# The experts' second layer in half-precision parts, and where its weights and the first biases are loaded

## The chip, the cores and the metric

The kernel runs on one core of one Trainium2 chip. The metric is device time in microseconds (us) of one execution, as the median of several. The engines are TensorE (PE; PEld is its weight load), VectorE (DVE), ScalarE (ACT), GpSimd (POOL) and SyncE (SP), which here only issues DMAs.

## The reference

Rows of 256 numbers (3327 of them, padded to 26 tiles of 128) pass through an attention over an adjacency matrix, a feed-forward with a capacity per expert, an aggregation over the same adjacency, and a layer of eight experts, of which every row uses two. Each part reads a normalised x and adds to x. What matters here is the last layer:

```python
def _L1_ffn_ref(x, Wg, bg, W1, b1, W2, b2):
    B, S, D, DFF, E, K = (4, 1024, 256, 512, 8, 2)
    logits = jnp.einsum('bsd,de->bse', x, Wg) + bg
    topk_vals, topk_idx = jax.lax.top_k(logits, K)
    topk_w = jax.nn.softmax(topk_vals, axis=-1)
    ...
    h = jnp.einsum('bsd,edf->bsef', x, W1) + b1
    a, g = jnp.split(h, 2, axis=-1)
    act = jax.nn.silu(a) * g
    expert_out = jnp.einsum('bsef,efd->bsed', act, W2) + b2
    return jnp.einsum('bse,bsed->bsd', weights_per_expert, expert_out)
```

## The kernel before

Four stretches follow each other on the core. **Attention** fills 0 to 405 us and is not touched. **`capacity_ffn`** fills 405 to 624 us. It is written out as slots: in slots 0 to 51 (chunk c is slot // 4, 13 chunks of two 128-row tiles' work) every engine does its part of the feed-forward, and from slot 32 on a `row_work(slot)` is placed between, which normalises x, turns it and projects it (`project_row`, `turn_rows`, `normalise_row`, `row_moments`); slots 52 to 68 hold row work alone, one row tile a slot. On the side this stretch finds a scale for the experts' first weights: ACT loads each expert's W1 (`expert_load`, 1024 KB) into the buffers `W` that are free by then and squares it with a sum (`expert_square`, L926), one expert in each of chunks 2 to 9; the largest sum gives `w_scale` near the end (`expert_sums` at slot 60, `expert_scales` at slot 63).

**`aggregation_and_experts`** opens with the aggregation, 624 to about 795 us: 44 products a row tile in half precision, fed by large loads of the adjacency and of the expert weights. ACT issues the loads of the experts' W2 (`weight_load`), SP those of the first biases b1, two each at i = 20, 22 and 24 of 26, and the rest with b2 behind them. Then each row is scattered to two slots of a table in DRAM (`slot_rows`, on POOL), and 59 tiles of 128 slots are read back.

The **expert tile loop** (820 us to the end) works on three tiles at once. Its order is each engine's own code, `iteration(s, u)`, with semaphores between; tiles 0 to 5 and the last are unrolled, those between run in a loop of two tiles a round, whose turn (a branch) falls into every other tile. In iteration s

- PE does the first layer of tile s (12 products of 512 columns, L1597, "hid"), turns the rows of tile s+1 (L1586), turns the activations of tile s-1 (L1607) and does the second layer of tile s-2 (L1617), which is in fp32: four products, each recorded as two instructions;
- DVE computes `weight` and `place_i` for tile s-3 (L1762, L1765), takes hid into `hb` with the bias (L1769), makes the rest xT_lo of tile s+1 (L1753), and multiplies `act = silu * gate` (L1776);
- ACT makes xT_hi of tile s+1 (L1460), copies the turned activations of tile s-1 out of PSUM (L1469), computes silu (L1473) and tanh (L1474) of tile s, and scales the bias and the output of tile s-3 (L1479, L1482);
- POOL adds those two (L1837) and stores 128 rows by index, adding to the output in DRAM (L1842); each such store waits for the one before it to land.

In the profile many buffers of this block carry the name of the memory they lie in: `X`, `own_H`, `adj_room`, `PS`.

Of the kernel before, what the change touches and what calls it, by code (L numbers as in the profile page):

```python
# [7 lines left out]
ALU = mybir.AluOpType  # L8
# [630 lines left out]
def capacity_ffn(nc, t, dram):  # L639


    with ExitStack() as ctx:
# [59 lines left out]
        held = [w1, w2]  # L702
        eps = sb("eps", [P, 1])
        e_sq, e_sum = sb("e_sq", [P, E1]), sb("e_sum", [P, 1])
        e_root, e_floor, e_rec = (sb(n, [P, 1]) for n in ("e_root", "e_floor", "e_rec"))
        e_in = [sem(f"c_ein{u}") for u in range(2)]
        e_squared, e_summed = sem("c_esq"), sem("c_esum")
        e_rooted, e_scaled = sem("c_eroot"), sem("c_escale")
        wsn_in, wsn_hi, wsn_lo, wsn_scaled = sem("c_wsn"), sem("c_wsnhi"), sem("c_wsnlo"), sem("c_wsnscale")
# [10 lines left out]
        SLOTS, SUMS_AT = PROJECT_AT + T, 60  # L720
# [5 lines left out]
        def pair_at(slot, offset):  # L726
            return [(slot - offset) // 2] if 0 <= slot - offset < T and (slot - offset) % 2 == 0 else []

# [5 lines left out]
        def _(sp):  # L734
# [15 lines left out]
            sp.wait_ge(later_in, 80)  # L750

# [22 lines left out]
        def _(pe):  # L774
# [83 lines left out]
            def project_row(i):  # L858
                r, s = i // 2, i % 2
                if i == 0:  # L860
                    pe.wait_ge(keep_done, len(GR))
                    pe.wait_ge(wsn_lo, 1)
# [9 lines left out]
            for slot in range(SLOTS):  # L872
# [14 lines left out]
                    if slot == SUMS_AT:  # L887
                        pe.wait_ge(y_taken, NCH - 1)
                        pe.wait_ge(e_squared, E1)
                        nc.tensor.matmul(psY[NCH % 2][:, 0:E1], unit[:, :], e_sq[:, :], start=True,  # L890
                                         stop=True).then_inc(e_summed, 1)
# [12 lines left out]
        def _(act):  # L904
# [10 lines left out]
            def expert_load(e):  # L915
                if e < 2:
                    act.wait_ge(w_lo, e + 1)
                else:
                    act.wait_ge(e_squared, e - 1)
                act.dma_start(held[e % 2][:, :, :].rearrange("p k n -> p (k n)"),  # L920
                              dram["eW1"][:, e, :]).then_inc(e_in[e % 2], 16)

            def expert_square(e):
                act.wait_ge(e_in[e % 2], 16 * (e // 2) + 16)
                flat = held[e % 2][:, :, :].rearrange("p k n -> p (k n)")
                nc.scalar.activation(flat, flat, ACT.Square, accum_out=e_sq[:, e:e + 1]).then_inc(e_squared, 1)  # L926

# [18 lines left out]
            def row_work(slot):  # L946
# [4 lines left out]
                for g, (_, b) in enumerate(RG):  # L951
                    if slot == ROWS_AT + b + 1:
                        row_deviation(g)

# [40 lines left out]
            for c in range(NCH):  # L995
# [17 lines left out]
                gelu_hi(c, 2)  # L1013
                row_work(4 * c + 2)
# [5 lines left out]
            for slot in range(4 * NCH, SLOTS):  # L1020
                row_work(slot)
                if slot == SUMS_AT + 2:
                    act.wait_ge(e_scaled, 1)
                    nc.scalar.activation(e_root[:, :], e_sum[:, :], ACT.Sqrt).then_inc(e_rooted, 1)

        @block.vector
        def _(dve):
# [60 lines left out]
            def row_work(slot):  # L1088
# [9 lines left out]
                for i in row_at(slot, ROWS_AT + 1):  # L1098
                    row_moments(i)

            def expert_sums():
                dve.wait_ge(e_summed, 1)
                v.tensor_reduce(e_sum[:, :], psY[NCH % 2][:, 0:E1], AX_X, ALU.max).then_inc(e_scaled, 1)

            def expert_scales():
                dve.wait_ge(e_rooted, 1)
                v.tensor_scalar(e_floor[:, :], e_root[:, :], TINY, None, ALU.max).then_inc(e_scaled, 1)
                dve.wait_ge(e_scaled, 2)
                v.reciprocal(e_rec[:, :], e_floor[:, :]).then_inc(e_scaled, 1)
                v.tensor_scalar(t["w_unscale"][:, :], e_floor[:, :], 1.0 / (FULL * H_SCALE), None, ALU.mult).then_inc(e_scaled, 1)  # L1110
                dve.wait_ge(e_scaled, 4)
                v.tensor_scalar(t["w_scale"][:, :], e_rec[:, :], FULL, None, ALU.mult).then_inc(e_scaled, 1)
# [144 lines left out]
            for slot in range(4 * NCH, SLOTS):  # L1257
# [5 lines left out]
                if slot == SUMS_AT:  # L1263
                    expert_sums()
                if slot == SUMS_AT + 3:
                    expert_scales()


def aggregation_and_experts(nc, t, dram, out):


    with ExitStack() as ctx:
# [40 lines left out]
        W2 = room[:, 0:E1 * KF * D].rearrange("p (e k d) -> p e k d", e=E1, k=KF)  # L1313
# [6 lines left out]
        actT = [carve(KF * P).rearrange("p (k n) -> p k n", k=KF) for _ in range(2)]  # L1320
# [34 lines left out]
        weight_waits = sem("f_weight_waits")  # L1355
# [582 lines left out]
```

## Time and profile before

| | |
|---|---|
| median of three executions | 1146.9 us (1146.87, 1149.44, 1146.9) |
| profiled execution, its own time | 1146.19 us |
| its span | 1144.4 us |
| busy: PE, DVE, ACT, POOL | 1020.9, 757.1, 610.4, 354.6 us |
| granted clock of PE, mean | 0.949 of full |

The span is the time between the first and the last recorded instruction; the execution's own time has 1.8 us more around it. Busy times add up the instructions of an engine, so an engine with a low share can still be the one that all wait for in one stretch.

### The profile page before, as it was taken

To read this page: it belongs to the slowest core of one execution; us is meant where nothing else is said; L and a number is where in the kernel's file an instruction comes from. 1 tells how busy PE (TensorE), PEld (TensorE's weight loads), DVE (VectorE), ACT (ScalarE), POOL (GpSimd) and SP (SyncE) were. 2 spreads that over 40 slices of the span, in tenths; PEclk is the share of its full clock that TensorE was granted. 3 is DMA by queue.
4 is the path that set the end of the run, shared out by engine and by line. 5 is a ranking of instruction groups with operands and counts; after the bars stand their busy time and mean duration, and the time that the engine had idled before them with its cause. 6 is when DMAs were issued, how large, how long until landed. Compare 5 with 4: busy or idle time off the path is not lost. (4 is left out here: it accounts for less than half of the span.)

```text
span 1144.4 us, 23391 instructions
## 1 busy us (share of the span) xinstructions
PE 1020.9 (89%) x7604; PEld 821.5 (72%) x7605; DVE 757.1 (66%) x1636; ACT 610.4 (53%) x923; POOL 354.6 (31%) x337
## 2 busy tenths in 40 slices
PE   5749999999999699798987999998399999999991
PEld 4539989998999579687754888887166666666661
DVE  5599999999993364865665566766355555555550
ACT  2767878787873477767642212112145555555541
POOL 0233232222322000009231044433224444444443
PEclk9759999999999689999999999999599999999996
DMA  9998787878720311220061799998523333333322
GB/s 373 243 287 251 229 254 223 256 223 260 221 87 1 115 74 38 80 81 26 1 119 47 186 241 239 243 244 264 215 38 52 55 55 48 53 55 55 48 45 23
DMA packets 72845, 161.64 MB, mean 141 GB/s; under 512 B 7376, under 2 KB 58960, under 8 KB 66768
## 3 DMA queue, kind: packets, MB, share of 16 engines
q1 hardware_dynamic: 48928, 97.85, 26.9%
q0 software_dynamic: 18128, 40.17, 20.0%
q10 hardware_dynamic: 5728, 22.81, 5.5%
q8 instruction: 38, 0.62, 0.2%
q14 instruction: 23, 0.19, 0.1%
HBM read 137.47 MB, written 45.49 MB: 160 GB/s over the span
## 5 line engine op out<-in xcount | busy, mean ns | idle before, releaser
L577 PE MATMUL PS<-G,PT 128*128 128x256 f16 x2028 | 234.4, 273 | 0.0
L577 PEld LDWEIGHTS PS<-G,PT 128*128 128x128 f16 x2028 | 198.9, 98 | 22.5
L1597 PE MATMUL PS<-W,X 128*128 x708 | 164.1, 382 | 4.3 <-DVE X L1753 4.3
L1769 DVE SCALAR_TENSOR_TENSOR own_H<-PS,w_unscale,own_H 128x1024 f32<-128x1024 f32 x59 | 75.7, 1284 | 97.8 <-PE PS L1597 97.8
L1597 PEld LDWEIGHTS PS<-W,X 128*128 128x128 f16 x708 | 69.5, 98 | 84.0 <-issue 7.4
L1523 PE MATMUL PS<-own_H,adj_room 128*128 128x256 f16 x572 | 129.3, 272 | 0.0
L1521 PE MATMUL PS<-own_H,adj_room 128*128 128x257 f16 x572 | 129.3, 273 | 0.0
L1617 PE MATMUL PS<-adj_room,X 128*128 x472 | 111.6, 380 | 0.2 <-issue 0.2
L561 PE MATMUL PS<-ident,probs 128*128 128x128 f32 x676 | 91.8, 283 | 21.1 <-ACT probs L321 15.8
L406 DVE SCALAR_TENSOR_TENSOR score<-S2low,S1low,S2row 128x3327 f32<-128x3327 f32 x25 | 106.5, 4260 | 0.0
L1842 POOL DMA_INDIRECT out_dram<-X,place_i x59 | 92.3, 1564 | 28.1 <-POOL X L1837 19.9
L561 PEld LDWEIGHTS PS<-ident,probs 128*128 128x128 f32 x676 | 79.1, 146 | 26.6 <-issue 17.6
L310 ACT CAST PT<-PS 128x1024 f16<-128x1024 f32 (+1 forms) x78 | 61.9, 795 | 62.8 <-PE PS L561 62.8
L424 DVE CUSTOM_DVE_ANT_0 score<-score,maskbias 128x3327 f32<-128x3327 f32 x25 | 90.6, 3625 | 5.4 <-DVE score L406 5.2
L1837 POOL TENSOR_TENSOR X<-X 128x256 f32<-128x256 f32 x59 | 44.3, 751 | 159.5 <-ACT X L1482 152.5
L1617 PEld LDWEIGHTS PS<-adj_room,X 128*128 128x128 f32 x472 | 85.1, 190 | 9.7 <-issue 0.4
L1460 ACT ACTIVATE X<-PS 128x256 f16<-128x256 f32 x59 | 22.7, 384 | 123.2 <-PE PS L1586 123.2
L321 ACT ACTIVATE probs<-score,shift_by 128x3327 f32<-128x3327 f32 x26 | 79.9, 3073 | 8.3 <-POOL shift_by L254 8.3
L1050 DVE SCALAR_TENSOR_TENSOR c_G_lo<-c_G,c_g_scale,c_G_hi 128x512 f16<-128x512 f32 x52 | 41.2, 793 | 61.8 <-ACT c_G_hi L967 61.6
L430 DVE TENSOR_TENSOR PT<-PS,PT 128x1024 f16<-128x1024 f32 (+1 forms) x78 | 73.2, 943 | 10.1 <-ACT PT L310 10.1
L316 ACT ACTIVATE maskbias<-adjf,big 128x3327 bf16<-128x3327 f32 x26 | 79.9, 3074 | 0.0
L800 PE MATMUL c_psH<-W 128*128 128x256 f16 x624 | 78.9, 278 | 0.0
(280 smaller groups left out, 1854.4 us busy)
## 6 DMA issues: line engine op xcount, KB each, us to landing
adjf<-adj_dram SPq DMA_DIRECT2D x26, 1664.0 KB, 8.0
slot_rows<-blank SPq DMA_DIRECT2D x26, 1032.0 KB, 11.1
adj_room<-adjT_dram POOLq DMA_DIRECT2D x22, 832.0 KB, 10.5
W<-eW_dram ACTq DMA_DIRECT2D x8, 1024.0 KB, 4.7
adj_room<-eW_dram ACTq DMA_DIRECT2D x8, 1024.0 KB, 9.3
X<-slot_rows SPq DMA_DIRECT2D x59, 129.0 KB, 2.5
own_H<-eb_dram SPq DMA_DIRECT2D x8, 512.0 KB, 5.9
adj_room<-eW_dram ACTq DMA_DIRECT2D x8, 512.0 KB, 8.7
```

The lines of the kernel that those rows point to most:

```text
L316: nc.scalar.activation(bias[u][:, 0:N], adjf[u][:, 0:N], ACT.Relu, bias=big[:, :], scale=-EDGE_SCALE).then_inc(mask_ready, 1)
L321: nc.scalar.activation(probs[u][:, 0:N], score[u][:, 0:N], ACT.Exp, bias=shift_by[u][:, :], accum_out=total[u][:, :]).then_inc(probs_ready, 1)
L406: v.scalar_tensor_tensor(score[u][:, 0:N], S2low[:, 0:N], S1low[:, ds(t, 1)], S2row[:, 0:N], ALU.add, ALU.max).then_inc(leaky_ready, 1)
L424: v.tensor_tensor_reduce(score[u][:, 0:N], score[u][:, 0:N], bias[u][:, 0:N], 1.0, -2 * FAR, ALU.subtract, ALU.max, rowmax[u][:, :]).then_ ...
L561: mm = nc.tensor.transpose(psT[g % 3][:, (j - a) * P:(j - a + 1) * P], probs[u][:, j * P:(j + 1) * P], ident[:, :])
L577: mm = nc.tensor.matmul(acc[u][:, 0:D], left, right, start=(j == 0 and n == 0), stop=(j == T - 1 and n == 2))
L800: mm = nc.tensor.matmul(psH[b % 2][:, (m % 2) * CH:(m % 2 + 1) * CH], w1p[left][:, k, m * P:(m + 1) * P], HT[right][:, k, c * CH:(c + 1) * ...
L1521: nc.tensor.matmul(acc[u][:, 0:D + 1], left, H[:, j, 0:D + 1], start=(j == 0), stop=False, skip_group_check=True)
L1523: mm = nc.tensor.matmul(acc[u][:, 0:D], left, H[:, j, D + 2:2 * D + 2], start=False, stop=(j == T - 1), skip_group_check=True)
L1597: mm = nc.tensor.matmul(psHE[u][:, n * F1:(n + 1) * F1], left[u][:, k, :], W1[:, e, k, part, n * F1:(n + 1) * F1], start=(m == 0), stop=(m ...
L1617: mm = nc.tensor.matmul(psY[u][:, 0:D], actT[u][:, k, :], W2[:, e, k, :], start=(k == 0), stop=(k == KF - 1))
L1842: pool.indirect_dma_start(out=out, in_=ys[u][:, :], in_offset=None, out_offset=bass.IndirectOffsetOnAxis(ap=place_i[:, s:s + 1], axis=0), ...
```

## The change

It has three parts.

1. In the expert tile loop the second layer is done in half-precision parts: W2 and the activations are each a sum of two f16 numbers, and y = hi·hi + lo·hi + hi·lo is 12 products of 256 columns in place of four in fp32. For the activations' range each row of a tile is divided by its own size: ACT squares `hb` with a sum, DVE turns that into `size` and `rsize`, act is multiplied by `rsize`, DVE makes the rest `actT_lo`, and the output is scaled by `y_scale` (weight times size) in place of `weight`.
2. In `capacity_ffn` ACT also loads and squares W2 (four loads of two experts), two loads and squares a chunk in chunks 2 to 7; the scales are found at slots 36 to 43; and W2 of the eight experts is split into its two parts (`second_weight_hi` on ACT at slot 45 + 3e, `second_weight_lo` on DVE one slot later, the last at slot 67), which SP stores to DRAM, 512 KB each. SP waits for those stores before the stretch ends.
3. In the aggregation b1 is loaded one expert at a time at i = 2, 6, 10, 14, 18 and 22; W2 is read from the parts, in as many bytes.

```diff
+        E_LOADS = E1 + E1 // 2
...
-        SLOTS, SUMS_AT = PROJECT_AT + T, 60
+        SLOTS, SUMS_AT, SPLIT_AT = PROJECT_AT + T, 36, 45
...
+            sp.wait_ge(e_squared, E_LOADS)
+            for e in range(2):
+                sp.dma_start(raw2[e], dram["eW2"][:, e, :, :].rearrange("p k d -> p (k d)")).then_inc(raw2_in[e], 16)
+            for e in range(E1):
+                u = e % 2
+                sp.wait_ge(second_lo, e + 1)
+                sp.dma_start(dram["W2_parts"][:, e, :, :], parts2[u][:, :, :]).then_inc(parts2_out[u], 16)
+                if e + 2 < E1:
+                    sp.dma_start(raw2[u], dram["eW2"][:, e + 2, :, :].rearrange("p k d -> p (k d)")).then_inc(raw2_in[u], 16)
+            for u in range(2):
+                sp.wait_ge(parts2_out[u], 16 * (E1 // 2))
...
+            def second_weight_hi(e):
+                act.wait_ge(raw2_in[e % 2], 16 * (e // 2) + 16)
+                act.wait_ge(e_scaled, 5)
+                wait(act, parts2_out[e % 2], 16 * (e // 2))
+                nc.scalar.activation(parts2[e % 2][:, 0, :], raw2[e % 2], ACT.Copy,
+                                     scale=t["w2_scale"][:, :]).then_inc(second_hi, 1)
...
-                if 2 <= c < 2 + E1:
-                    expert_square(c - 2)
-                if 3 <= c < 1 + E1:
-                    expert_load(c - 1)
+                if 2 <= c < 2 + E_LOADS // 2:
+                    expert_square(2 * c - 4)
                 gelu(c, 2)
                 gelu_hi(c, 1)
                 row_work(4 * c + 1)
                 gelu(c, 3)
                 gelu_hi(c, 2)
+                if 2 <= c < 2 + E_LOADS // 2:
+                    expert_square(2 * c - 3)
...
+            def second_weight_lo(e):
+                dve.wait_ge(second_hi, e + 1)
+                v.scalar_tensor_tensor(parts2[e % 2][:, 1, :], raw2[e % 2], t["w2_scale"][:, :], parts2[e % 2][:, 0, :],
+                                       ALU.mult, ALU.subtract).then_inc(second_lo, 1)
...
-                if i >= 20:
-                    for e in range(i - 20, i - 18):
-                        sp.dma_start(b1[:, e, :], dram["eb1"][:, e, :]).then_inc(b1_in, 16)
+                if i % 4 == 2:
+                    e = i // 4
+                    sp.dma_start(b1[:, e, :], dram["eb1"][:, e, :]).then_inc(b1_in, 16)
...
+                    nc.scalar.activation(squares, hb[u][:, :], ACT.Square, accum_out=sumsq[u][:, :]).then_inc(squared, 1)
                     nc.scalar.activation(silu[u][:, :], hb[u][:, 0:F1], ACT.Silu).then_inc(silu_ready, 1)
...
-                    settled(act, weight_waits, (y_ready, s - 2))
+                    settled(act, weight_waits, (y_ready, s - 2), (y_scaled, s - 2))
                     nc.scalar.activation(yw[1 - u][:, :], psY[1 - u][:, 0:D], ACT.Copy,
-                                         scale=weight[:, ds(s - 3, 1)]).then_inc(yw_ready, 1)
+                                         scale=y_scale[:, ds(s - 3, 1)]).then_inc(yw_ready, 1)
...
                     for k in range(KF):
-                        mm = nc.tensor.matmul(psY[u][:, 0:D], actT[u][:, k, :], W2[:, e, k, :], start=(k == 0),
-                                              stop=(k == KF - 1))
+                        for n, (left, part) in enumerate(((actT_hi, 0), (actT_lo, 0), (actT_hi, 1))):
+                            mm = nc.tensor.matmul(psY[u][:, 0:D], left[u][:, k, :], W2[:, e, part, k, :],
+                                                  start=(k == 0 and n == 0), stop=(k == KF - 1 and n == 2))
...
+                    dve.wait_ge(weighed, s - 2)
+                    dve.wait_ge(size_kept, s - 2)
+                    v.tensor_tensor(y_scale[:, ds(s - 3, 1)], weight[:, ds(s - 3, 1)], sizes[:, ds(s - 3, 1)],
+                                    ALU.mult).then_inc(y_scaled, 1)
...
+                if due(s - 1):
+                    dve.wait_ge(actT_ready, s)
+                    wait(dve, y_ready, s - 3)
+                    v.tensor_tensor(actT_lo[1 - u][:, :, :].rearrange("p k n -> p (k n)"), psA[:, :],
+                                    actT_hi[1 - u][:, :, :].rearrange("p k n -> p (k n)"), ALU.subtract).then_inc(actT_lo_ready, 1)
...
+                    dve.wait_ge(squared, s + 1)
+                    v.tensor_scalar(size[u][:, :], sumsq[u][:, :], 1.0 / (2 * FULL), TINY * TINY, ALU.mult,
+                                    ALU.max).then_inc(sized, 1)
+                    dve.wait_ge(sized, s + 1)
+                    v.reciprocal(rsize[u][:, :], size[u][:, :]).then_inc(act_scaled, 1)
                     dve.wait_ge(silu_ready, s + 1)
+                    dve.wait_ge(act_scaled, s + 1)
                     wait(dve, a_turned, s - 1)
-                    v.tensor_tensor(act_sb[u][:, :], silu[u][:, :], hb[u][:, F1:2 * F1], ALU.mult).then_inc(act_ready, 1)
+                    v.scalar_tensor_tensor(act_sb[u][:, :], silu[u][:, :], rsize[u][:, :], hb[u][:, F1:2 * F1], ALU.mult,
+                                           ALU.mult).then_inc(act_ready, 1)
+                    v.tensor_scalar(sizes[:, ds(s, 1)], size[u][:, :], t["w2_unscale"][:, :], None, ALU.mult).then_inc(size_kept, 1)
```

The order of DVE's instructions in one tile of the expert tile loop, before: `own_H` is hb or its target, the first `X` under it xT_lo, the last act.

```order
L1762 TENSOR_SCALAR weight<-balance 128x1
L1765 TENSOR_SCALAR place_i<-kept 128x1
L1769 ISA
L1769 SCALAR_TENSOR_TENSOR own_H<-PS,w_unscale,own_H 128x1024
L1751 TENSOR_SCALAR kept<-X 128x2
L1753 SCALAR_TENSOR_TENSOR X<-PS,X 128x256
L1776 TENSOR_TENSOR X<-X,own_H 128x512
```

And in the changed kernel, the same engine and the same place:

```order
L1815 TENSOR_SCALAR weight<-balance 128x1
L1818 TENSOR_SCALAR place_i<-kept 128x1
L1821 TENSOR_TENSOR y_scale<-weight,sizes 128x1
L1826 ISA
L1826 SCALAR_TENSOR_TENSOR own_H<-PS,w_unscale,own_H 128x1024
L1804 TENSOR_SCALAR kept<-X 128x2
L1806 SCALAR_TENSOR_TENSOR X<-PS,X 128x256
L1833 TENSOR_TENSOR X<-PS,X 128x512
L1837 TENSOR_SCALAR size<-sumsq 128x1
L1840 RECIPROCAL rsize<-size 128x1
L1844 SCALAR_TENSOR_TENSOR X<-X,rsize,own_H 128x512
L1846 TENSOR_SCALAR sizes<-size,w_unscale 128x1
```

One small operation stands ahead of hb, three operations between xT_lo and act, and one behind act.

ACT's instructions in one tile of the same loop, before: the first two `X` are xT_hi and the activations' copy, the third is silu.

```order
L1460 ACTIVATE X<-PS 128x256
L1469 COPY X<-PS 128x512
L1473 ACTIVATE X<-own_H 128x512
L1474 ACTIVATE balance<-kept 128x1
```

And in the changed kernel:

```order
L1511 ACTIVATE X<-PS 128x256
L1520 CAST X<-PS 128x512
L1524 ACTIVATE rows,sumsq<-own_H 128x1024
L1525 ACTIVATE X<-own_H 128x512
L1526 ACTIVATE balance<-kept 128x1
```

The square of all 1024 columns of hb stands between hb and silu.

DVE's instructions at slots 58 and 59 of `capacity_ffn`, before: `own_H` are projected rows, `c_r_h` is a normalised row on its way to PE, `c_rowT_lo` a turned one.

```order
L1083 SCALAR_TENSOR_TENSOR own_H<-c_psR,own_H 128x256
L1085 SCALAR_TENSOR_TENSOR own_H<-c_psR,c_own_back,c_own_bias 128x256
L1069 RECIPROCAL c_row_rstd<-c_row_std 128x2
L1073 TENSOR_SCALAR c_r_h<-X,c_moments,c_row_rstd 128x256
L1061 BN_STATS stats<-X 128x6
L1063 BN_AGGR c_moments<-stats 128x2
L1083 SCALAR_TENSOR_TENSOR own_H<-c_psR,own_H 128x256
L1085 SCALAR_TENSOR_TENSOR own_H<-c_psR,c_own_back,c_own_bias 128x256
```

And in the changed kernel, where the lower part of one expert's W2 stands between the two slots:

```order
L1118 SCALAR_TENSOR_TENSOR own_H<-c_psR,own_H 128x256
L1120 SCALAR_TENSOR_TENSOR own_H<-c_psR,c_own_back,c_own_bias 128x256
L1104 RECIPROCAL c_row_rstd<-c_row_std 128x2
L1108 TENSOR_SCALAR c_r_h<-X,c_moments,c_row_rstd 128x256
L1096 BN_STATS stats<-X 128x6
L1098 BN_AGGR c_moments<-stats 128x2
L1160 SCALAR_TENSOR_TENSOR W<-W,w_scale 128x1024
L1118 SCALAR_TENSOR_TENSOR own_H<-c_psR,own_H 128x256
L1120 SCALAR_TENSOR_TENSOR own_H<-c_psR,c_own_back,c_own_bias 128x256
```

DVE has one operation more, and the next slot's two projected rows come behind it.

## Rows read from the trace of the kernel before

**Rows 1.** Windows: busy us (x instructions) of PE, PEld, DVE, ACT, POOL; clock, DMA share, GB/s

```profile
900.00:950.00 50.00, 50.00 (x263) 33.15 (x262) 26.84 (x60) 25.64 (x60) 23.09 (x21) 1.00 0.34 53
```

**Rows 2.** The chain that ended last, 899 to 912: start, us, what

```profile
901.22 1.73 PE PS L1617 x8
902.95 2.59 PE PS L1597 x12
905.54 0.22 PE PS L1586 x2
905.76 0.44 PE PS L1607 x4
```

**Rows 3.** Timeline of PE and DVE at the loop's start, tiles 0 to 2

```profile
822.05 4.36 PE L1597 MATMUL PS<-W,X 128*128 x12 [1.25 <-DVE X L1753]
...
831.32 1.28 DVE L1769 SCALAR_TENSOR_TENSOR own_H<-PS,w_unscale,own_H 128x1024 f32<-128x1024 f32 x1 [2.07 <-PE PS L1597]
...
836.06 1.28 DVE L1769 SCALAR_TENSOR_TENSOR own_H<-PS,w_unscale,own_H 128x1024 f32<-128x1024 f32 x1 [2.07 <-PE PS L1597]
```

**Rows 4.** Timeline of DVE, then ACT, two tiles of the loop

```profile
900.72 1.28 DVE L1769 SCALAR_TENSOR_TENSOR own_H<-PS,w_unscale,own_H 128x1024 f32<-128x1024 f32 x1 [1.63 <-PE PS L1597]
902.70 0.69 DVE L1776 TENSOR_TENSOR X<-X,own_H 128x512 f32<-128x512 f32 x1 [0.30 <-ACT X L1473]
904.06 0.15 DVE L1762 TENSOR_SCALAR weight<-balance  x1 [0.67 <-issue]
905.79 1.28 DVE L1769 SCALAR_TENSOR_TENSOR own_H<-PS,w_unscale,own_H 128x1024 f32<-128x1024 f32 x1 [1.41 <-PE PS L1597]
907.86 0.69 DVE L1776 TENSOR_TENSOR X<-X,own_H 128x512 f32<-128x512 f32 x1 [0.38 <-ACT X L1473]
908.72 0.15 DVE L1762 TENSOR_SCALAR weight<-balance  x1 [0.17 <-issue]
910.67 1.28 DVE L1769 SCALAR_TENSOR_TENSOR own_H<-PS,w_unscale,own_H 128x1024 f32<-128x1024 f32 x1 [1.63 <-PE PS L1597]
...
902.04 0.63 ACT L1473 ACTIVATE X<-own_H 128x512 f32<-128x512 f32 x1 [0.19 <-DVE own_H L1769]
```

**Rows 5.** The chain that ended last, 600 to 640: one product of 256 columns

```profile
626.43 0.11 PE PS L1521
```

**Rows 6.** Timeline of ACT: a square with its sum, and the operation behind it

```profile
460.71 1.90 ACT L926 ACTIVATE W<-W 128x2048 f32<-128x2048 f32 x1
...
462.60 0.56 ACT L959 ACTIVATE c_G<-c_psH,c_b,c_w_back 128x256 f32<-128x256 f32 x1
```

**Rows 7.** Timeline of POOL: the last stores of the loop

```profile
1124.17 1.56 POOL L1842 DMA_INDIRECT out_dram<-X,place_i  x1 [2.74 <-DMA out_dram<-X,place_i]
...
1128.74 1.56 POOL L1842 DMA_INDIRECT out_dram<-X,place_i  x1 [2.25 <-DMA out_dram<-X,place_i]
```

**Rows 8.** Groups of instructions: busy us, mean ns, idle before

```profile
L1152 DVE SCALAR_TENSOR_TENSOR W<-W,c_w_scale 128x2048 f16<-128x2048 f32 x2 | 4.7, 2346 | 0.8 <-ACT W L988 0.8
```

**Rows 9.** Timeline of DVE in the slots of row work, and the next block's first

```profile
609.34 0.42 DVE L1083 SCALAR_TENSOR_TENSOR own_H<-c_psR,own_H 128x256 f16<-128x256 f32 x1 [1.15 <-ACT own_H L943]
...
622.75 0.48 DVE L1085 SCALAR_TENSOR_TENSOR own_H<-c_psR,c_own_back,c_own_bias 128x256 f32<-128x256 f32 x1
624.41 0.06 DVE L1629 MEMSET eps<- 128x1 f32 x1 [1.18 <-PEq L71]
```

**Rows 10.** DMA issues: KB each, median us to landing

```profile
W<-eW_dram ACTq DMA_DIRECT2D x8, 1024.0 KB, 4.7
X<-slot_rows SPq DMA_DIRECT2D x59, 129.0 KB, 2.5
```

**Rows 11.** Windows as in rows 1, in the feed-forward's chunks and the row work

```profile
450.00:460.00 10.00, 10.00 (x94) 9.09 (x94) 3.02 (x5) 6.68 (x13) 0.00 (x0) 1.00 0.12 48
...
600.00:620.00 20.00, 15.24 (x76) 7.27 (x75) 15.84 (x47) 6.70 (x18) 2.37 (x4) 1.00 0.00 1
```

**Rows 12.** The chain that ended last, 800 to 840: the hand-over's scatter

```profile
811.53 5.36 DMA slot_rows<-rows,slot_i
```

More of the change, by code:

```diff
@@ L708, in capacity_ffn @@
         e_rooted, e_scaled = sem("c_eroot"), sem("c_escale")
+        raw2_in, parts2_out = ([sem(f"c_{n}{u}") for u in range(2)] for n in ("raw2", "parts2"))
+        second_hi, second_lo = sem("c_second_hi"), sem("c_second_lo")
         wsn_in, wsn_hi, wsn_lo, wsn_scaled = sem("c_wsn"), sem("c_wsnhi"), sem("c_wsnlo"), sem("c_wsnscale")
@@ L727, in pair_at, with split_at @@
             return [(slot - offset) // 2] if 0 <= slot - offset < T and (slot - offset) % 2 == 0 else []
+        def split_at(slot):
+            e = (slot - SPLIT_AT) // 3
+            return [e] if slot >= SPLIT_AT and (slot - SPLIT_AT) % 3 == 0 and e < E1 else []
         def fronts(c):
@@ L953, in row_work @@
                         row_deviation(g)
+                if slot == SUMS_AT + 5:
+                    act.wait_ge(e_scaled, 2)
+                    nc.scalar.activation(e_root[:, :], e_sum[:, :], ACT.Sqrt).then_inc(e_rooted, 1)
+                for e in split_at(slot):
+                    second_weight_hi(e)
             def gelu(c, b):
@@ L1099, in row_work @@
                     row_moments(i)
+                if slot == SUMS_AT + 1:
+                    expert_sums()
+                if slot == SUMS_AT + 7:
+                    expert_scales()
+                for e in split_at(slot - 1):
+                    second_weight_lo(e)
             def expert_sums():
                 dve.wait_ge(e_summed, 1)
[L1103 removed]
+                v.tensor_reduce(e_sum[:, 0:1], psR[0][:, 0:E1], AX_X, ALU.max).then_inc(e_scaled, 1)
+                v.tensor_reduce(e_sum[:, 1:2], psR[0][:, E1:E_LOADS], AX_X, ALU.max).then_inc(e_scaled, 1)
             def expert_scales():
@@ L1319, in aggregation_and_experts @@
         silu, act_sb = ([carve(F1) for _ in range(2)] for _ in range(2))
-        actT = [carve(KF * P).rearrange("p (k n) -> p k n", k=KF) for _ in range(2)]
+        actT_hi, actT_lo = ([carve(KF * P, F16).rearrange("p (k n) -> p k n", k=KF) for _ in range(2)] for _ in range(2))
+        squares = rows[:, :, :, :, :].rearrange("p q u k n -> p (q u k n)")[:, 0:2 * F1]
+        sumsq, size, rsize = ([sb(f"{n}{u}", [P, 1]) for u in range(2)] for n in ("sumsq", "size", "rsize"))
+        sizes, y_scale = sb("sizes", [P, NS]), sb("y_scale", [P, NS])
         yw, bw, ys = ([carve(D) for _ in range(2)] for _ in range(3))
```

63 lines of the change are left out of this document (35 added, 28 removed).

## The prediction

> **What bounds the kernel now.** I read the page's engines and slices first, then windows over each stretch, then in each the chain of what released what, and last the timelines of the engines that meet there. The change touches three of the four stretches.
>
> In the expert tile loop PE is never idle: 50.00 us of the window's 50, at full granted clock [rows 1]. The chain that ended last is PE's own order, tile after tile: 1.73 for the second layer, 2.59 for the first, 0.22 and 0.44 for the turns, 4.98 us a tile [rows 2]. The reader should see that this is a full PE and not a stall. But two loops through other engines run beside it, nearly as long, and they are found only by adding up starts.
>
> Loop one: hb, xT_lo of the next tile, its first layer, its hb. At the start, where tile 2's iteration has only just begun to add a second layer and PE is idle before hb for nothing but this, hb follows hb after 836.06 - 831.32 = 4.74 us [rows 3]. It holds DVE's 1.8 and PE's first layer and nothing of the second layer, so no cheaper second layer shortens it.
>
> Loop two: hb, silu, act, the small operations for tile s-3, hb. Two hb lie 910.67 - 900.72 = 9.95 us apart for two tiles, 4.97 a tile, and before each DVE waited for PE, 1.41 and 1.63 us [rows 4]. So loop two has a slack of about 1.5 us a tile: its own length is 3.66 in the tile that carries the loop's turn and 3.25 in the other.
>
> In `capacity_ffn`'s chunks PE is full too, with ACT busy 6.68 of 10 us [rows 11]. In its last slots it is not: PE 15.24 of 20, DVE 15.84 of 20 [rows 11], and DVE's only idle time is some 1.15 us in every pair of row tiles, ahead of one projected row [rows 9]. The end of the stretch is set by DVE's last row at 622.75 + 0.48, and the next block starts at 624.41 [rows 9]. In the hand-over after the aggregation the chain runs through scatters that take 5.36 us each [rows 12] while the DMA engines are busy.
>
> **The tile loop, part by part.** *Removed:* 1.73 us a tile of fp32 products [rows 2]. *Added on PE:* 12 products of 256 columns at the 0.11 us at which one follows the other on the chain [rows 5], 1.32 us. PE's own work becomes 2.59 + 0.22 + 0.44 + 1.32 = 4.57 us, 0.41 less; over 56 tiles that would be 23 us. I don't believe it, because loop one is 4.74 and allows 0.23.
>
> *Added on loop two.* The square of 1024 columns stands ahead of silu. Between a silu of 512 columns, 0.63 us [rows 4], and a square of 2048, 1.90 [rows 6], a column costs 0.00083, so 1024 take 1.05. The operation behind the 2048-wide square starts 462.60 - 460.71 = 1.89 after it, its sum being read in between [rows 6], so silu moves 1.04 us back. Then, behind act, one small operation (`sizes`), and behind `place_i` another (`y_scale`, which waits for `weight` just ahead of it): each like `weight` at 0.15 [rows 4], some 0.15 to 0.17 from start to start.
>
> To the 3.66 and 3.25 come 1.04, 0.15, 0.17 and 0.15 for the start of hb behind the last small operation, which PE's wait covered before and no row shows (I take one more small operation): 5.17 in the tile with the loop's turn, 4.76 in the other. The second is loop one's length, so either may set that tile. The pair takes 5.17 + 4.76 = 9.93, against 9.95. The whole gain of PE is eaten: PE will wait some 0.4 us a tile, for DVE.
>
> The three further operations on DVE between xT_lo and act cost nothing: `actT_lo` is 512 columns from PSUM, some 0.7 us like act itself [rows 4], and with `size` and `rsize` ends about when silu does (silu started 1.32 after hb [rows 4] and now ends near hb + 1.32 + 1.04 + 0.63 = 2.99; xT_lo ends at about hb + 1.7, plus 0.7 is 2.4, and size and rsize take 0.3). This cover has 0.3 us in it; if it is gone, act is late by what is missing, in every tile. The xT path, `hi`, is ahead of the square on ACT and stays hidden. yw of tile s-3 is now behind the square on ACT too; only at the last tile does somebody wait for it: +1.0 us once. The unrolled tiles at the start have no turn and gain up to 0.2 each, -1.3 together; 25 pairs at -0.02 give -0.5. Sum -0.8, and an error of 0.05 in a tile is worth 2.5 us over the 25 pairs. I take **0 for the tile loop**. Bounds: -12.6 + 1 (loop two stays hidden and loop one sets the pace, 0.23 x 55 tiles less), and +12 (both 0.2 us longer than I think, 0.2 x 56, plus the last tile).
>
> POOL's stores take 1128.74 - 1124.17 = 4.57 us each when nothing else holds them [rows 7], each waiting for the landing of the one before. That is the same as PE's new 4.57, so they would bound the loop there, and not at 4.75.
>
> **The feed-forward's part.** *Squares:* four more of 1.9 us [rows 6], with ACT idle 3.3 us in 10 and PE full [rows 11]: 0, at most 0.5 each if an extra square makes the next gelu late. In return the chunks 8 and 9 have none, and the row work behind can begin earlier by at most one square, 1.90; I take -0.8. *Splits:* DVE's `lo` of 1024 columns. The nearest row is 2048 columns at 2346 ns [rows 8]; half of it and some 0.1 for the part that doesn't shrink is 1.28. Eight of them are 10.2 us. DVE has 1.15 us free in a pair of row tiles and a split comes every third tile, so most of those behind slot 57 fill the idle time ahead of a projected row; the two that fall while DVE has no idle time (e = 3 and 4, slots 55 to 58) are paid in full, 2 x 1.28 = +2.6. Bounds 0 and +6 (five of them). *Stores:* the last `lo` comes at slot 67 of 68, so ends just before DVE's last row at 623.23 [rows 9]. Behind it SP issues 512 KB and the block waits for the landing. In the trace 1024 KB land after 4.7 us and 129 KB after 2.5 [rows 10], so 512 KB after 3.3, and the wait, the issue and the last split's delay add some 0.4: +3.7. Bounds +2 and +5. Together +5.5.
>
> **The aggregation's part.** 1 MB less is behind the last scatter's queue. Between 129 KB in 2.5 us and 1024 KB in 4.7 [rows 10], 1 MB itself is some 2.5 us; the scatters at 5.36 us [rows 12] have that traffic beside them, but only half of the transfers stand ahead of them. I take -1.3, bounds 0 and -2.5 (all of it). At i = 2 to 22 the loads add to full DMA engines while PE is full; 0. W2 is read in as many bytes: 0.
>
> **The sum**, on the profiled execution's own 1146.19: 0 + 5.5 - 1.3 = +4.2, 1150.4. The median of the runs is 0.7 above that execution, so 1151.
>
> **A rule of the skill that speaks against the change.** PE has no idle time in the loop now and the clock is full [rows 1]; the first tile's 12 products, for which PE had waited 1.25 us after the idle hand-over, took 4.36 us in place of 2.59 [rows 2, 3]. If idle time in the loop brought that level back, a tile would cost 1.77 more, +99 us over 56 tiles. Against it: between 600 and 620 us PE was busy 15.24 of 20 and the clock stayed at 1.00 [rows 11], and I expect 4.57 of 4.96 busy here. The Trainium skill, "TensorE: Matmul & The Clock Gate", section "What's actually happening", says that a monitor sets the gate by how busy the PE has been recently, between 1.2 and 2.4 GHz. By that rule, making PE's work shorter while the pace stays can lose the clock; the rows of 600 to 620 show that a busy share well under this one did not.
>
> **The rivals.**
> - *Loop two stays hidden* (0.23). If the turn of the loop overlaps what I count as serial, loop one sets every tile: -11.6 + 5.5 - 1.3 = -7.4, 1139.5. For it: a third of DVE's 1.36 before `weight` is "issue" [rows 4], which may shrink where other work fills it. Against: it is work of DVE's own sequencer.
> - *PE stays the bound* (0.05): 4.57 a tile, -22.6 + 1 + 4.2 = -17.4, 1129.5. It needs loop one to be shorter than at the start; nothing shows that.
> - *Loop two is worse than I think* (0.18), the one on the other side of what the second layer is worth: size and rsize end behind silu, or small operations cost 0.25 in place of 0.15. From +0.05 us a tile on the loop is slower than before. At +0.2: 12 + 4.2, 1163.
> - *The feed-forward's part is hidden* (0.08): splits fall into idle time, the last store lands under the block's end, tile loop 0: 1146.19 - 1.3 + 0.7 = 1145.6. The change then is none that can be measured.
> - *The clock falls* (0.04): in a third of the tiles +33, 1184.
> - My forecast (0.42): 1151, own range 1146 to 1157.
>
> **How the numbers follow.** A measurement here tells some 0.3% (3.4 us) from no change: 1143.5 to 1150.3. Of the forecast's 0.42, 0.17 lie within and 0.25 above. Faster: 0.23 + 0.05 = 0.28. Same: 0.17 + 0.08 = 0.25. Slower: 0.25 + 0.18 + 0.04 = 0.47. The range 1138 to 1163 takes in the first rival and most of the third, and leaves out PE as the bound, the clock, and a half of the third's far end, under 0.2.
>
> **What would show it.** PE in the window 900 to 950 busy about 46 of 50 with DVE ahead of its waits; hb to hb 5.17 and 4.75 in turn; the second layer 1.3 us a tile; silu 2.4 after hb; POOL waiting for yw. In the feed-forward, two splits without idle time around slot 55 to 58, and 3 to 4 us between DVE's last row and the next block's first instruction where there is 1.18 now. In the hand-over, shorter scatters. The prediction is wrong if hb to hb in the turn's tile is under 5.0 or over 5.4, or if the block's end does not move.

## The result, and the profile after

The changed kernel takes 1165.93 us in the median of four executions (1164.01 to 1167.02), the kernel before 1146.88 (1145.3 to 1149.44). The ratio is 1.0162, with a 95% interval of 1.0139 to 1.0186: 18.6 us slower. The prediction said 1151, with 1138 to 1163.

The changed kernel's profiled execution took 1166.48 us, its span is 1164.7 us against 1144.4. The page's head:

```profile
span 1164.7 us, 24836 instructions
PE 1006.9 (86%) x7840; PEld 803.1 (69%) x7841; DVE 846.3 (73%) x1942; ACT 680.9 (58%) x1057; POOL 357.6 (31%) x337
```

PE has 14.0 us less work and the span is 20.3 us longer, so the time is in waits. To find where, I noted the start of the same instruction in both traces at the ends of each stretch. First DVE at the end of the feed-forward, in the changed kernel, to be read beside [rows 9]:

```profile
629.83 0.48 DVE L1120 SCALAR_TENSOR_TENSOR own_H<-c_psR,c_own_back,c_own_bias 128x256 f32<-128x256 f32 x1
633.64 0.06 DVE L1682 MEMSET eps<- 128x1 f32 x1 [3.33 <-PEq L71]
```

The last row ends at 630.31, 7.1 us later than before, and the next block's first instruction comes 3.33 us behind it in place of 1.18: 2.2 more.

The 7.1 are not lost in the row work alone. DVE takes the output of every chunk of the feed-forward out of PSUM, and the start of this instruction can be compared in both traces. Its last start ahead of the first split of a W2, before and after, with that split on ACT:

```profile
551.55 0.72 DVE L1055 SCALAR_TENSOR_TENSOR own_H<-c_psY,c_y_back,c_b 128x512 f32<-128x512 f32 x1
```

```profile
554.74 0.74 DVE L1090 SCALAR_TENSOR_TENSOR own_H<-c_psY,c_y_back,c_b 128x512 f32<-128x512 f32 x1
...
562.24 1.13 ACT L958 ACTIVATE W<-W,w_scale 128x1024 f16<-128x1024 f32 x1
```

That is 3.2 us late already, of which 0.2 come from ahead of the feed-forward (its first product starts at 405.26, before at 405.05). At the same instruction of the last chunk, 603.76 and 598.27, it is 5.5, and at the last row 7.1. So 3.0 are lost before any split, where the change adds loads and squares of W2, and 3.9 behind the first split. PE's products say the same: the first of the eleventh chunk starts 127.4 us behind the first of the stretch, in place of 124.3.

Then the chain that ended last through the hand-over, before and after:

```profile
795.66 4.61 issue
...
822.05 4.38 PE PS L1597 x12
```

```profile
810.36 4.61 issue
...
826.23 3.25 DMA slot_rows<-rows,slot_i
...
834.68 5.03 PE PS L1649 x12
```

From the block's start to the 4.61 the aggregation takes 171.25 us before and 176.72 after: 5.5 more. From there to the first tile's products it is 26.39 before and 24.32 after, 2.1 less, and the last scatter alone, 3.25 in place of 5.36 [rows 12], is 2.1 shorter. At the other end, hb of the last tile starts at

```profile
1114.61 1.29 DVE own_H L1769
```

before, and after at

```profile
1134.27 1.29 DVE own_H L1826
```

so the loop takes 299.6 us from its first product in place of 292.6: 7.0 more. What is left behind it is 0.6. The sum is 7.1 + 2.2 + 5.5 - 2.1 + 7.0 + 0.6 = 20.3.

The aggregation's 5.5 lie in three windows (columns as in [rows 1]), the first at its start and two in the middle:

```profile
633.60:643.60 10.00, 9.68 (x70) 7.81 (x71) 1.83 (x8) 2.00 (x1) 2.20 (x4) 0.79 0.94 249
703.60:713.60 10.00, 8.69 (x77) 7.46 (x75) 6.12 (x23) 3.50 (x5) 5.67 (x5) 0.97 1.06 246
713.60:723.60 10.00, 10.00 (x83) 8.30 (x82) 6.92 (x38) 1.01 (x3) 2.00 (x3) 0.86 0.95 241
```

In the first, PE's granted clock was 0.79 of full where it was 1.00 before; in the last it was 0.86. Both are times at the lower of the clock's two levels, 1.2 GHz in place of 2.4; in the first window they add up to some 4 us. Ahead of the first dip PE had stood idle:

```profile
633.92 0.40 PE L1573 MATMUL PS<-own_H,W 128*128 128x257 f16 x1 [5.51 <-DVE running L1684]
```

The kernel before waited 2.73 us at this place. The products that the dip covers follow each other at 0.21 us, where the full clock gives 0.11:

```profile
634.32 0.21 PE PS L1575
634.53 0.21 PE PS L1573
```

**The tile loop.** A window of it, and two tiles on PE and DVE with the starts that matter:

```profile
920.00:970.00 50.00, 46.06 (x296) 29.54 (x295) 39.69 (x107) 34.87 (x80) 22.32 (x20) 1.00 0.33 53
```

```profile
921.89 2.76 PE L1649 MATMUL PS<-W,X 128*128 x12
...
925.14 1.47 PE L1670 MATMUL PS<-adj_room,X 128*128 x12
927.30 2.76 PE L1649 MATMUL PS<-W,X 128*128 x12 [0.69 <-issue]
```

```profile
920.06 1.28 DVE L1826 SCALAR_TENSOR_TENSOR own_H<-PS,w_unscale,own_H 128x1024 f32<-128x1024 f32 x1 [0.64 <-PE PS L1649]
923.17 0.75 DVE L1844 SCALAR_TENSOR_TENSOR X<-X,rsize,own_H 128x512 f32<-128x512 f32 x1 [0.17 <-ACT X L1525]
924.80 1.28 DVE L1826 SCALAR_TENSOR_TENSOR own_H<-PS,w_unscale,own_H 128x1024 f32<-128x1024 f32 x1
926.06 0.42 DVE L1806 SCALAR_TENSOR_TENSOR X<-PS,X 128x256 f16<-128x256 f32 x1
930.30 1.28 DVE L1826 SCALAR_TENSOR_TENSOR own_H<-PS,w_unscale,own_H 128x1024 f32<-128x1024 f32 x1 [0.64 <-PE PS L1649]
```

Two tiles take 930.30 - 920.06 = 10.24 us, where they took 9.95 [rows 4]. The clock is full. The reader should look at the two idle marks. DVE waits 0.64 for PE before the third hb, and PE itself waited 0.69 before the first layer that this hb needs, for "issue": for nothing that another engine did. What it needed, xT_lo, was there at 926.06 + 0.42 = 926.48. So the wait is in PE's own instruction stream, which reads numbers, sets addresses and turns the loop between the products. The trace has these under the line that wrote them (PEldq is PE's stream; count, duration in ns, start of the first and last); the reading of an expert number and the loop's branch, from 923 to 928:

```profile
L1421 PEldq FUSED_REGOPS  x3: 42/151/151, 924.0 to 926.7; - x3
L1421 PEldq TENSOR_LOAD <-expert x2: 299/301/303, 924.1 to 926.4; - x2
...
L47 PEldq COMPARE_BRANCH  x1: 208/208/208, 926.0 to 926.0; - x1
```

The first of these instructions starts at 924.0, right behind act's end at 923.92: in PE's code the wait for act stands ahead of it. From there the stream needs 3.3 us until 927.30: a reading (0.9), eight address operations for the twelve products (1.0), the branch and a second reading (1.4), all one after the other. This is a third loop, over two tiles: hb 920.06, act's end 923.92 (3.86), PE's stream until 927.30 (3.38), the first layer and hb at 930.30 (3.00), together 10.24.

### The profile page after: what moved, and what is told of

The parts are those of the page before. It is cut to its first block and busy times, and to the rows that moved or that the text cites. A ratio compares the mean times of both kernels' runs of the same rounds, so it can differ in the third digit from the quotient of the medians.

```text
span 1164.7 us, 24836 instructions
## 1 busy us (share of the span) xinstructions
PE 1006.9 (86%) x7840; PEld 803.1 (69%) x7841; DVE 846.3 (73%) x1942; ACT 680.9 (58%) x1057; POOL 357.6 (31%) x337
## 5 line engine op out<-in xcount | busy, mean ns | idle before, releaser
L1670 PE MATMUL PS<-adj_room,X 128*128 x708 | 88.4, 276 | 0.2 <-issue 0.2
L834 PE MATMUL c_psY<-W,c_G_hi 128*128 128x256 f16 x416 | 72.9, 277 | 6.3 <-DVE c_G_lo L1085 6.3
```

What stands on the lines that cost most here:

```text
L1670: mm = nc.tensor.matmul(psY[u][:, 0:D], left[u][:, k, :], W2[:, e, part, k, :], start=(k == 0 and n == 0), stop=(k == KF - 1 and n == 2))
```

## The experiments

In the first four, run on one chip, the kernel before took 1145.9 us.

**e1_early_load** moves one statement in PE's code:

```diff
+                if due(s - 2):
+                    e = tile_expert(pe, s - 2)
                 if due(s - 1):
                     pe.wait_ge(act_ready, s)
...
                 if due(s - 2):
-                    e = tile_expert(pe, s - 2)
```

> PE reads the expert number of tile s-2 before it waits for act, in place of behind that wait; nothing else changes. Theory A (a loop over two tiles through PE's own instruction stream sets the pace: act, then PE's reading of an expert number, its address operations, the turn of the loop and a second reading, then the first layer, hb, act): some 0.8 us less in each pair of tiles, 25 pairs, so about 1147 to 1152 against 1166. Theory B (loop two of the prediction, through DVE and ACT alone, sets the pace): no change, 1166.

Measured: 1149.54 us, ratio 1.0036 (1.0022 to 1.0050), 16 us less than the changed kernel by the two medians and 14 by the two ratios, which allow for the kernel before having been faster here. In its trace hb starts at

```profile
912.29 1.28 DVE L1827 SCALAR_TENSOR_TENSOR own_H<-PS,w_unscale,own_H 128x1024 f32<-128x1024 f32 x1 [0.15 <-issue]
917.03 1.28 DVE L1827 SCALAR_TENSOR_TENSOR own_H<-PS,w_unscale,own_H 128x1024 f32<-128x1024 f32 x1
922.05 1.28 DVE L1827 SCALAR_TENSOR_TENSOR own_H<-PS,w_unscale,own_H 128x1024 f32<-128x1024 f32 x1 [0.15 <-issue]
```

4.74 and 5.02 us apart, 9.76 for two tiles: 0.48 less, some 12 us over 25 pairs, and now DVE waits for PE ahead of none of them. Theory A is borne out and B, that DVE and ACT alone set 10.24, falls. This is also the prediction's loop two, laid bare: it had said 5.17 and 4.76. The first product of the loop starts at 829.65, not at 834.68: another 5 us between these two executions lie ahead of the loop, with one dip of the clock in place of two. That part isn't the edit's, since nothing there was changed.

**e2_square_256** shortens the square to 256 of the 1024 columns, with the constant of the mean to match:

```diff
-nc.scalar.activation(squares, hb[u][:, :], ACT.Square, accum_out=sumsq[u][:, :])
+nc.scalar.activation(squares[:, 0:D], hb[u][:, 0:D], ACT.Square, accum_out=sumsq[u][:, :])
```

> The square in the tile loop covers 256 of hb's 1024 columns (it leaves out the size's other columns). By the rows a column costs 0.00083 us, so it is 0.64 us shorter. Theory A: the loop over two tiles holds one square, so a pair is 0.64 shorter, 16 us over the loop: 1150. Theory B: 0.64 less in every tile until loop one's 4.74 or PE's 4.57 holds: 1148 at best. Theory C (the square costs nothing by itself, the loss is elsewhere): 1166.

Measured: 1148.87 us, ratio 1.0024 (1.0014 to 1.0034). Two of its tiles take 922.62 - 912.85 = 9.77 us:

```profile
912.85 1.28 DVE L1826 SCALAR_TENSOR_TENSOR own_H<-PS,w_unscale,own_H 128x1024 f32<-128x1024 f32 x1 [0.55 <-PE PS L1649]
914.45 0.68 DVE L1833 TENSOR_TENSOR X<-PS,X 128x512 f16<-128x512 f32 x1
915.48 0.75 DVE L1844 SCALAR_TENSOR_TENSOR X<-X,rsize,own_H 128x512 f32<-128x512 f32 x1
922.62 1.28 DVE L1826 SCALAR_TENSOR_TENSOR own_H<-PS,w_unscale,own_H 128x1024 f32<-128x1024 f32 x1 [0.54 <-PE PS L1649]
```

The pair lost 0.47, not 0.64: act starts 2.63 behind hb in place of 3.11, because now DVE's own order (actT_lo, size, rsize, each right behind the other) holds it. 0.48 earlier for act, 0.47 less for the pair: one act in a loop of two tiles, as A says. Under B each of the two tiles would have lost it.

**e3_four_products** keeps `((actT_hi, 0),)` of the three terms. 

> The second layer keeps four of its twelve products (hi by hi alone; the two rests are left out). PE has 0.88 us less work a tile, and 4 address operations in its stream in place of 9. Theory A: only the address operations count, 5 x 0.125 = 0.6 us a pair, 1151. Theory B: no change, 1166. If PE's own work were the bound: 0.88 a tile, below 1120.

(The trace of the changed kernel shows eight address operations a tile for the twelve products, not nine, and four for the kernel before.)

Measured: 1149.37 us, ratio 1.0037 (1.0026 to 1.0048). Two tiles, and the window of the loop:

```profile
908.78 1.28 DVE L1826 SCALAR_TENSOR_TENSOR own_H<-PS,w_unscale,own_H 128x1024 f32<-128x1024 f32 x1
...
918.55 1.28 DVE L1826 SCALAR_TENSOR_TENSOR own_H<-PS,w_unscale,own_H 128x1024 f32<-128x1024 f32 x1
```

```profile
910.00:960.00 50.00, 38.97 (x222) 22.74 (x223) 41.23 (x114) 36.01 (x83) 23.36 (x21) 1.00 0.33 53
```

The pair takes 9.77 us, as in e1_early_load, and again DVE waits for PE ahead of no hb: in both, loop two is what is left. A third of the second layer's products do no better than all twelve with the number read early. PE is busy 38.97 of 50 and nobody gains by it. The clock stays at 1.00 in this window, at a lower busy share than in the changed kernel. The rule cited in the prediction, from the Trainium skill, "TensorE: Matmul & The Clock Gate", section "What's actually happening", that the gate follows how busy PE has been, shows no effect here.

**e4_before_square** adds to the kernel before

```diff
+                    nc.scalar.activation(squares, hb[u][:, :], ACT.Square, accum_out=sumsq[u][:, :])
                     nc.scalar.activation(silu[u][:, :], hb[u][:, 0:F1], ACT.Silu).then_inc(silu_ready, 1)
```

> The kernel before, with the square of 1024 columns (with its sum) ahead of silu and nothing else. Theory A: the loop over two tiles was about 8.3 us long in the kernel before and becomes 9.3, under PE's 9.95: no change, but for 1 us at the last tile: 1147 to 1148. Theory C turned round (the square is itself what costs, in whichever kernel): +7 us, 1154.

Measured: 1146.93 us, ratio 1.0013 (1.0000 to 1.0026), 1.5 us. In its window PE is full, with ACT at 34.92 in place of 25.64:

```profile
900.00:950.00 50.00, 50.00 (x265) 33.27 (x263) 26.94 (x61) 34.92 (x80) 22.91 (x21) 1.00 0.35 53
```

The square is free as long as PE's array has work queued ahead. It costs only with the other edits.

In the next four, on another chip, the kernel before took 1145.57 us.

**e5_split_two** puts the splits at slots 45 + 2e:

```diff
-            e = (slot - SPLIT_AT) // 3
+            e = (slot - SPLIT_AT) // 2
```

> The split of one expert's W2 comes every second slot from slot 45 on, in place of every third: the last lower part is at slot 60 of 68 and its store lands long before the block ends. Theory D (9.2 us are lost at the end of the feed-forward: the splits on DVE take some 7 and the last store's landing some 2.2, and while PE waits for it its clock falls, another 2): the wait before the next block goes from 3.3 to about 1.2 us and the next block's first products run at the full clock: 4 us less, 1162. Rival (the wait is hidden by something else that ends as late): 1166.

Measured: 1164.83 us, ratio 1.0164 (1.0148 to 1.0180). Not the 4 us that D had. The wait at the block's end did shrink, to 1.23, but the last row ended at 635.66:

```profile
635.19 0.47 DVE L1120 SCALAR_TENSOR_TENSOR own_H<-c_psR,c_own_back,c_own_bias 128x256 f32<-128x256 f32 x1
636.89 0.06 DVE L1682 MEMSET eps<- 128x1 f32 x1 [1.23 <-PEq L71]
```

and ACT, with the rows behind it, had to wait for a W2 that was read back while the DMA engines were 0.98 busy:

```profile
602.16 1.15 ACT L958 ACTIVATE W<-W,w_scale 128x1024 f16<-128x1024 f32 x1 [3.27 <-DMA W<-eW_dram]
...
580.00:600.00 20.00, 15.50 (x91) 10.19 (x92) 13.18 (x30) 9.29 (x15) 10.29 (x12) 0.83 0.98 211
```

In this window POOL's early loads of the adjacency (832 KB each, from slot 52 on) run beside the stores and the reading of W2, whose 512 KB land after 11.5 us; which of them makes the other late was not tried apart. So earlier splits gained the store's landing and lost more in the rows.

**e6_b1_back** has the changed kernel with b1 loaded at i = 20, 22, 24, and **e7_b1_only** the kernel before with b1 loaded at i = 2 to 22; each edit is that of the diff above, in one or the other direction.

> The changed kernel with the loads of b1 where they were before, two each at i = 20, 22 and 24. If the moved loads shortened the hand-over by 2 us and cost nothing in the aggregation: 1168. If they made the aggregation's adjacency and weight loads late, by the 1.5 us for which no clock accounts: 1166 to 1167, nothing to be seen.

> The kernel before with only the loads of b1 moved to i = 2 to 22. By the prediction's term: 1.3 us less (0 to 2.5), 1144.6 beside 1145.9. Rival (the added traffic in the aggregation gives it back): 1146.

Measured: e6_b1_back 1163.23 us, ratio 1.0157 (1.0141 to 1.0173), which can't be told from the changed kernel, although in its trace the way from the 4.61 to the first tile's products is 26.36 us again. e7_b1_only 1143.65 us, ratio 0.9981 (0.9970 to 0.9991): 2 us faster, and the one version here that beats both kernels. The last scatter is the place, first in e6_b1_back, then in e7_b1_only:

```profile
820.99 5.28 DMA slot_rows<-rows,slot_i
```

```profile
809.58 3.13 DMA slot_rows<-rows,slot_i
```

**e8_early_and_two** is e1_early_load and e5_split_two together.

> The changed kernel with the early reading of the expert number in PE's stream and the splits every second slot. If the two gains add: 1149.5 - 4 = 1145.5, about the kernel before.

Measured: 1151.87 us, ratio 1.0052 (1.0036 to 1.0068). Against e5_split_two, on the same chip, the early reading is worth 13 us; the second edit is worth nothing, as in e5_split_two. The sum that was expected, 1145.5, did not come.

In the last four the kernel before took 1148.36 us on the chip, so ratios are to be compared, with 1.0162 for the changed kernel and 1.0036 for e1_early_load.

**e9_small_behind** moves, on top of e1_early_load, the three operations of DVE for tile s-3:

```diff
-                if due(s - 3):
-                    dve.wait_ge(balanced, s - 2)
...
                 if due(s + 1):
                     rows_lo(s + 1, 1 - u)
+                if due(s - 3):
+                    dve.wait_ge(balanced, s - 2)
...
```

> The early reading of e1_early_load, and DVE's weight, place_i and y_scale for tile s-3 behind xT_lo in place of ahead of hb. Theory: with PE's stream out of the way, loop two (DVE and ACT) sets 4.89 us a tile in e1_early_load, and it holds these three small operations, some 0.5 us a tile; moved, the tile falls to loop one's 4.74: 0.15 x 50 = 7 us less than e1_early_load, 1142. Rival: they make size and rsize, and so act, later by as much: no change, 1149.5.

Measured: 1149.09 us, ratio 1.0003 (0.9987 to 1.0019). Two tiles take 918.98 - 909.32 = 9.66 us, 0.10 less than in e1_early_load, where 0.3 were expected:

```profile
909.32 1.28 DVE L1817 SCALAR_TENSOR_TENSOR own_H<-PS,w_unscale,own_H 128x1024 f32<-128x1024 f32 x1 [0.77 <-PE PS L1649]
914.23 1.28 DVE L1817 SCALAR_TENSOR_TENSOR own_H<-PS,w_unscale,own_H 128x1024 f32<-128x1024 f32 x1 [1.01 <-PE PS L1649]
918.98 1.28 DVE L1817 SCALAR_TENSOR_TENSOR own_H<-PS,w_unscale,own_H 128x1024 f32<-128x1024 f32 x1 [0.77 <-PE PS L1649]
```

DVE now waits for PE in every tile. One tile is at loop one's length (4.75 against 4.74), the other at 4.91. The tile loop of this version is about 0.29 us a pair faster than that of the kernel before, 7 us in all, and the version still only draws level, because of what stands ahead of the loop.

**e10_lo_on_pool** gives the lower parts of experts 4 to 7, whose upper parts now come at slots 57, 59, 61 and 63, to POOL, as a scaling and a subtraction.

> e1_early_load, with the lower part of W2 of experts 4 to 7 made on POOL in two operations, two slots apart, so that DVE has four splits less behind slot 57. Theory D1 (DVE's time sets the row work, each split behind slot 55 costs up to 1.25 us): 3 to 5 us less than e1_early_load, 1145 to 1146. D2 (ACT's upper part or the reloading through the two buffers is what delays the rows): no change, 1149.5.

Measured: ratio 1.0049 (1.0034 to 1.0064), no better than e1_early_load. One split takes POOL 5 us:

```profile
604.58 2.88 POOL L793 TENSOR_SCALAR W<-W,w_scale 128x1024 f32<-128x1024 f32 x1
607.54 2.13 POOL L795 TENSOR_TENSOR W<-W 128x1024 f16<-128x1024 f32 x1
```

It changes the splits' times and their engine together, so it decides nothing between D1 and D2.

**e11_lo_short** and **e12_both_short** shorten the operations and leave loads and stores:

```diff
-parts2[e % 2][:, 1, :], raw2[e % 2], ...
+parts2[e % 2][:, 1, 0:64], raw2[e % 2][:, 0:64], ...
```

> The changed kernel, but the lower part of each W2 covers 64 of 1024 columns (the rest of the lower part is zero, set once), so DVE's eight operations take 0.15 us in place of 1.25; all loads, stores and ACT's parts stay. D1: the row work ends some 6 to 7 us earlier, 1159. D2: unchanged, 1166.

> As e11_lo_short, and ACT's upper part covers 64 columns too (the rest is zero). What is left of the 7 us at the end of the row work against the kernel before then belongs to the loads, stores and the additional squares. D1: as e11_lo_short, 1159. If ACT's parts count: 1 to 3 us less than e11_lo_short.

Measured: e11_lo_short 1160.39 us, ratio 1.0088 (1.0054 to 1.0122); e12_both_short 1158.33 us, ratio 1.0074 (1.0052 to 1.0097). Against 1.0162 that is 8.5 us for the eight lower parts, with an interval of nearly 5 us to either side, and 1.6 us for the upper ones, which is within it. The first next-block instruction of e11_lo_short and of e12_both_short:

```profile
629.92 0.06 DVE L1684 MEMSET eps<- 128x1 f32 x1 [2.95 <-PEq L71]
```

```profile
626.40 0.06 DVE L1684 MEMSET eps<- 128x1 f32 x1 [2.95 <-PEq L71]
```

against 633.64 in the changed kernel: 3.7 and 3.5 in the order of the edits. So this pair of traces gives the lower parts less than the ratios do, and the upper ones, on ACT, as much; D1, which had DVE's time alone, expected no second step. How the two share it stays unsure. The same point lies at 624.41, 624.05 and 620.81 in the three traces with the earlier feed-forward (the kernel before, e4_before_square and e7_b1_only) and between 631.70 and 633.73 in the six with the changed one. Both edits also add two operations on DVE that set the buffers to zero ahead of the first split (0.91 us each in e12_both_short). No run took out the additional squares and loads, the other candidate.

## Why the prediction was wrong

- **What bounds the kernel** was read rightly, and loops one and two nearly so. "Loop one is 4.74": e9_small_behind has a tile of 4.75. Loop two was given as 5.17 and 4.76; e1_early_load, in which PE's stream no longer holds, shows 5.02 and 4.74. The square's 1.04 behind hb was right (silu starts 2.46 behind hb, at 922.52, predicted 2.4), and so was the claim that PE's gain would be eaten. But the tile with the loop's turn takes 5.50 us in the changed kernel, over the 5.4 that the prediction had named as a sign of being wrong.
- **The step that failed** is "I take 0 for the tile loop": the list of loops was not complete. The prediction counted PE as an array that works through 4.57 us a tile, and had no term for PE's own instruction stream. Before, that stream ran ahead of a full array and hid its readings, address operations and the loop's turn. The change takes 0.41 off the array, adds four address operations to the stream, and moves act, for which the stream waits, 1.1 us later. The stream then arrives behind the array, and the array stands 0.69 us. Shown by e1, e2, e3 and e4: taking 0.8 to 0.9 from the stream behind act, taking 0.48 from act, or taking address operations and products away each give back some 0.47 us of 10.24 (in e1 and e3 no more, because loop two holds from there), and the square without the rest costs nothing in the loop. Measured for the loop: +7.0, where the prediction had 0 and +12 as the bound. The rival "loop two is worse than I think" had the right sign and size and the wrong place; its mechanism (small operations of 0.25, late size and rsize) did not occur.
- **The squares** are a second step that failed: "-0.8", at most 0.5 each if one makes the next gelu late. The changed kernel is 3.0 us late before the first split. At the instruction compared above, and counted from the feed-forward's first product, the other traces with this code, e11 and e12 left out, are 1.3 to 4.1 us late; the three with the earlier feed-forward agree within 0.1. One place shows how: a second square stands ahead of an operation that leads, over DVE, to a turn for which PE then stands idle, in a window in which it was full before:

```profile
443.08 1.91 ACT L950 ACTIVATE W<-W 128x2048 f32<-128x2048 f32 x1
```

```profile
447.70 0.66 PE L802 MATMUL c_psT<-ident,c_r_h 128*128 128x128 f32 x4 [0.94 <-DVE c_r_h L120]
```

  ACT's idle 3.3 us in 10 was a mean and not room at that place. Whether the other 2 us are the squares too, or the loads beside them, is not shown.
- **The splits** were nearly of the right size: +2.6, bound +6, and from the first split to the last row 3.9 are lost. A split on DVE of 1.25 to 1.28 us is as long as was computed (a row of the changed kernel stands below), and DVE's idle time ahead of projected rows did take up a part: behind the last chunk its marks add up to 2.9 us in place of 5.3. What the prediction had no term for is ACT's upper part, for which e12_both_short has up to 3.5 us. By the ratios alone e11_lo_short would put 8.5 us, give or take nearly 5, on the lower parts.

```profile
617.43 1.28 DVE L1160 SCALAR_TENSOR_TENSOR W<-W,w_scale 128x1024 f16<-128x1024 f32 x1
```

- **The store's landing**, +3.7, was mis-sized the other way: 2.2.
- **The clock.** The prediction looked for a fall in the tile loop and found arguments against it, rightly. It did not look at the block's start, where PE's idle time grew from 2.73 to 5.51 us and the products behind it ran at the lower level, some 2 us. In the traces of all runs the eight waits of 4.5 to 5.5 us at this place are each followed by such a dip, and of the six waits of 2.7 to 2.8 us three are (e5_split_two, e7_b1_only, e10_lo_on_pool) and three are not. With the rule from the Trainium skill that is cited at e3_four_products the eight long waits agree; it does not tell which of the short ones has a dip. So the longer wait of the change comes with the dip each time, and the dip isn't tied to the change alone. The second dip, at 713 us, came in some executions and not in others. Of the aggregation's 5.5 us some 3.7 are the two dips and 1.3 are two longer waits of PE for ACT (1.31 us each where they were 0.67); what sets off the second dip and these waits stays open. The aggregation's own work isn't slower: from the block's start to the 4.61 it takes 171.3 us in the kernel before, in e4_before_square and in e8_early_and_two, which has the changed aggregation and no dip, and 172.8 to 173.3 in six traces with the first dip. The prediction had 0 here and no term for the wait at the boundary; of the 5.5 of the one profiled execution some 2 are in all of these six, and the rest came in some executions only.
- **b1**, -1.3 with -2.5 as the bound: right, -2.1 in the trace and 0.9981 in e7_b1_only.

The forecast's sum was 0 + 5.5 - 1.3. Measured it is 7.6 (loop and tail) + 9.3 (the feed-forward: 3.0 ahead of the splits, 3.9 behind the first, 2.2 for the landing, 0.2 from before it) + 5.5 (aggregation) - 2.1.

## What to carry to other kernels

Before giving an engine less array work, ask whether its instruction stream can keep ahead: count what it reads and computes between two products, and look at which wait stands ahead of it. A number that can be read before a wait should be: here that gave back 0.48 us of 10.24 and cost nothing. When the loops that one finds have lengths within a few per cent of each other, draw the one for every engine's stream as well, over as many turns as one wait reaches back. And an engine's mean idle time is not room for more work at every place: look at what waits for the operation that the new one is put ahead of. When a stretch ends late, compare the start of the same instruction at several points of it before naming the part that costs: here 3.0 us of 7.1 were lost ahead of the operations that looked like their cause.

## What the runs showed of the hardware

PE's stream takes some 1.4 us from the last address operation of one turn of the loop to the first product of the next (changed kernel, 925.9 to 927.30): 0.3 for the read of a number from memory, 0.2 for the branch, the rest in small register steps of up to 0.15 and what lies between them. DVE's branch took 0.056 us and PE's 0.208. POOL takes 2.88 us to scale 128x1024 numbers and 2.13 to subtract them, where DVE does both in 1.28. At the lower clock level products of 256 columns follow each other at 0.21 us, at the full one at 0.11.
